# Two bf16 remainders of the weighed values moved from VectorE to GpSimd in layers 1 and 2

## The chip, the cores and the metric

The kernel runs on one core of a Trainium2 chip. The time is the device time of one execution in microseconds (us). The engines are named as in the profile: PE (TensorE, with PEld for its weight loads), DVE (VectorE), ACT (ScalarE), POOL (GpSimd) and SP (SyncE, whose queue issues the DMAs).

## What is computed

Eight graphs of 1024 nodes with 128 features pass through four layers, each behind a normalisation and with its input added at the end. Layers 1 and 2 are graph attention with additive scores, 4 and 8 heads:

```python
h = jnp.maximum(_layernorm(x, axis=-1), 0.0)
x = x + _L1_gnn_ref(h, adj, L1_gnn_W, L1_gnn_a)
h = jnp.maximum(_layernorm(x, axis=-1), 0.0)
x = x + _L2_gnn_ref(h, adj, adj[None], L2_gnn_W, L2_gnn_a_src, L2_gnn_a_dst, L2_gnn_beta_tilde, L2_gnn_W_out)
...
Wh = jnp.einsum('bnf,hfd->bhnd', x, W)
e = ei[:, :, :, None] + ej[:, :, None, :]
e = jnp.where(e > 0, e, ALPHA * e)
e = jnp.where(adj[None, None] > 0, e, MASK_VAL)
att = jax.nn.softmax(e, axis=-1)
h = jnp.einsum('bhij,bhjd->bhid', att, Wh)
```

Layer 0 is attention with dot products, layer 3 attention with a bilinear score. Neither is touched.

## The kernel before

**The idea of layers 1 and 2.** The exponential of a leaky relu of a sum of two terms is one of two products of a factor per row and a factor per column; which of the two holds depends on the sign of the sum. So no score matrix is exponentiated. Per head a matrix `g` of fp8 marks where the sum is positive and an edge exists; PE multiplies `g` with the node values weighed by the column factors (L1032, into `acc`), and the edge matrix alone with the other weighing (L1014, into `post`). The weighed values are float32, and PE reads them as three bf16 parts that sum to the float32 value: the upper half of the word, the upper half of what is left, and the upper half of what is left after that. They lie in `parts`, two buffers `parts0` and `parts1`, for graphs in turn.

**The steps that make the parts.** `dve_weigh` (L1143, L1145) writes part 0 and raises `vals_ready`. `dve_rest` (L1149) writes part 1, which is part 0 less its bf16 half, and raises `rest_ready`. `dve_last_rest` (L1153) writes part 2 in the same way from part 1 and raises `parts_ready`, on which PE waits ahead of the first head of the next graph. Each of the two is one subtraction over 128 x 2112 elements in layer 1 and 128 x 2176 in layer 2, float32 from one input, every second bf16 from the other, all in SBUF.

**The order of the work.** Each engine has its own order, written by hand in `additive_layers`: a loop over graphs, in it a loop over heads `h`, and between heads numbered slots, two per head. The tables `soon` and `later` say which step of the next graph and of the one after it is done in which slot. On DVE a graph of layer 1 is: for each head, the marks of the head after it (`dve_head`: L1171, which makes one tile in layer 1 and two in layer 2, and two L1181, which combine with the edges), the sums of the head before it from PSUM (`dve_sums`, L1188, which free the four banks of `acc`), and the slots. `dve_weigh` stands in slot 4 (slot 6 in layer 2), the end of the graph before (`dve_combine`, L1205 to L1219) behind head 1, and `dve_base` (L1196, reads `post`) behind heads 2 to 4. ACT makes the other tiles of `g` (L1097), from rows `s_all` that SP loads; SP sends the load of a head once DVE has done L1171 of the head two before. PE may run a head into a bank of `acc` only once DVE has read the head before out of it.

**POOL** does little: per graph `pool_rstd` (L116, L118: the scale and offset of the normalisation two graphs ahead, for ACT's L125) and `pool_top` (L967: a maximum over all partitions, from `top_part`, for DVE's L1131). Between L967 and another kind of instruction stands an instruction that the order calls ISA.

## Time and profile before

| | us |
|---|---|
| median of 3 runs (lowest, highest) | 2028.11 (2024.01, 2032.48) |
| the profiled execution | 2026.8 |
| its span | 2024.6 |
| DVE busy | 1603.9, 79% |
| PE busy | 1650.5, 82% |
| ACT busy | 1339.6, 66% |
| POOL busy | 126.2, 6% |

The span is what the trace covers; the execution is 2.2 us longer. Layers 1 and 2 run from about 700 to 1640 us in the span. A busy share is an average over stages with different limits, and PE's is over modelled ends of pipelined matmuls. In a row of the timeline, the first number is the start and the second the time from the start of the first to the end of the last instruction of the row, whose count stands at the end; in square brackets is how long the engine was idle before it and who ended that. Single DVE instructions of a row overlap their neighbours by some hundredths of a microsecond.

### The profile page before, as it was taken

To read this page: it belongs to the slowest core of one execution; us is meant where nothing else is said; L and a number is where in the kernel's file an instruction comes from. 1 tells how busy PE (TensorE), PEld (TensorE's weight loads), DVE (VectorE), ACT (ScalarE), POOL (GpSimd) and SP (SyncE) were. 2 spreads that over 40 slices of the span, in tenths; PEclk is the share of its full clock that TensorE was granted. 3 is DMA by queue.
4 is the path that set the end of the run, shared out by engine and by line. 5 is a ranking of instruction groups with operands and counts; after the bars stand their busy time and mean duration, and the time that the engine had idled before them with its cause. 6 is when DMAs were issued, how large, how long until landed. Compare 5 with 4: busy or idle time off the path is not lost. (4 is left out here: it accounts for less than half of the span.)

```text
span 2024.6 us, 36872 instructions
## 1 busy us (share of the span) xinstructions
PE 1650.5 (82%) x13620; PEld 1056.3 (52%) x13620; DVE 1603.9 (79%) x2710; ACT 1339.6 (66%) x1751; POOL 126.2 (6%) x130
## 2 busy tenths in 40 slices
PE   3998988988986577999999777977797748999997
PEld 1444443434433356777777556755675534555554
DVE  4888988988987557888888889898888747666764
ACT  2766666666663576777776989888888814554553
POOL 1000010010000100000000000000000000000000
PEclk7999999999998688999999878888888869999999
DMA  8634634635622311111111112111211120000000
GB/s 232 160 102 122 141 92 115 147 89 127 141 71 68 119 43 39 47 43 42 50 46 43 54 64 74 65 64 55 74 65 64 63 89 1 11 22 10 10 11 21
DMA packets 74922, 146.49 MB, mean 72 GB/s; under 512 B 11937, under 2 KB 34722, under 8 KB 74754
## 3 DMA queue, kind: packets, MB, share of 16 engines
q1 hardware_dynamic: 74754, 144.23, 25.4%
q8 instruction: 108, 1.77, 0.4%
q14 instruction: 60, 0.49, 0.1%
HBM read 101.85 MB, written 8.78 MB: 55 GB/s over the span
## 5 line engine op out<-in xcount | busy, mean ns | idle before, releaser
L1097 ACT ACTIVATE g<-s_all,steep_d 128x1024 fp8e4<-128x1024 f32 x608 | 642.3, 1135 | 40.6 <-DMA s_all<-s_rows 20.6
L1032 PE MATMUL acc<-parts,g 128*128 128x102 bf16 (+1 forms) x6144 | 417.2, 229 | 24.7 <-DVE sums L1188 24.5
L1032 PEld LDWEIGHTS acc<-parts,g 128*128 128x128 fp8e4 x6144 | 401.5, 100 | 57.4 <-issue 40.5
L1014 PE MATMUL post<-parts,edge 128*128 128x396 bf16 (+1 forms) x1024 | 233.7, 384 | 88.4 <-DVE base L1196 88.4
L583 ACT ACTIVATE e<-s_ps 128x1024 f32<-128x1024 f32 x256 | 248.1, 1022 | 24.5 <-PE s_ps L439 22.3
L1181 DVE TENSOR_TENSOR g<-g,edge 128x1024 int32<-128x1024 int32 x192 | 228.1, 1220 | 34.1 <-ACT g L1097 34.1
L732 DVE SCALAR_TENSOR_TENSOR e<-e,bound 128x1024 f32<-128x1024 f32 x160 | 191.0, 1228 | 43.4 <-ACT e L583 43.3
L1014 PEld LDWEIGHTS post<-parts,edge 128*128 128x128 fp8e4 x1024 | 102.5, 102 | 195.9 <-issue 111.5
L435 PE MATMUL s_ps<-qs,ks 128*128 128x512 f32 x512 | 193.5, 487 | 6.6 <-DMA ks<-split 4.9
L451 PE MATMUL sum_ps<-e,pick 128*32 128x256 f32 x2048 | 142.2, 396 | 67.6 <-DVE e L732 57.4
L1879 ACT ACTIVATE z<-z,shift 128x1024 f32<-128x1024 f32 x64 | 73.6, 1149 | 161.0 <-DVE shift L1955 161.0
L589 ACT ACTIVATE chunk<-ctx_ps 128x512 f32<-128x512 f32 x128 | 76.2, 595 | 136.0 <-PE ctx_ps L460 136.0
L435 PEld LDWEIGHTS s_ps<-qs,ks 128*128 128x128 f32 x512 | 94.4, 197 | 128.2 <-issue 70.1
L1188 DVE TENSOR_REDUCE sums<-acc 128x132 f32<-128x396 f32 (+1 forms) x256 | 133.9, 569 | 27.3 <-PE acc L1032 27.2
L460 PE MATMUL ctx_ps<-e,v 128*32 128x512 f32 x1024 | 140.1, 620 | 0.0
L451 PEld LDWEIGHTS sum_ps<-e,pick 128*32 128x32 f32 x2048 | 54.7, 111 | 137.7 <-DVE e L732 68.2
L1948 DVE CUSTOM_DVE_ANT_0 z<-s_ps,bias 128x1024 f32<-128x1024 f32 x64 | 78.4, 1225 | 60.7 <-PE s_ps L1786 60.4
L1786 PE MATMUL s_ps<-ht,q 128*128 128x512 f32 x256 | 121.8, 598 | 4.9 <-DVE top L1948 3.8
L1808 PE MATMUL o_ps<-zt,h 128*128 128x512 f32 x256 | 117.9, 604 | 6.0 <-ACT zt L1884 6.0
L125 ACT ACTIVATE h<-x,offset,rstd 128x128 f32<-128x128 f32 (+1 forms) x256 | 101.8, 482 | 30.7 <-POOL offset L118 30.7
L1171 DVE TENSOR_SCALAR g<-s_all,minus_d 128x1024 fp8e4<-128x1024 f32 x160 | 114.3, 748 | 8.4 <-issue 3.2
L133 PE MATMUL aux<-ident,h 128*128 128x128 f32 x256 | 42.6, 322 | 80.2 <-ACT h L125 80.2
(158 smaller groups left out, 2146.7 us busy)
## 6 DMA issues: line engine op xcount, KB each, us to landing
s_all<-s_rows SPq DMA_DIRECT2D x96, 512.0 KB, 3.7
inv_all<-inv_rows SPq DMA_DIRECT2D x256, 128.0 KB, 2.9
qs<-split SPq DMA_DIRECT2D x128, 128.0 KB, 3.2
ks<-split SPq DMA_DIRECT2D x128, 128.0 KB, 2.8
x<-in_x SPq DMA_DIRECT2D x8, 512.0 KB, 6.8
inv_rows<-inv SPq DMA_DIRECT2D x32, 128.0 KB, 1.8
adj_in<-in_adj SPq DMA_DIRECT2D x8, 512.0 KB, 4.1
out_x<-x SPq DMA_DIRECT2D x8, 512.0 KB, 3.2
```

The costliest lines, as they stand in the source:

```text
L435: ins = pe.matmul(s_ps[:, hp, j, :], ks[par][:, 2 * hp + j, jt * P:(jt + 1) * P], qs[par][:, 2 * hp + j, half * HALF:(half + 1) * HALF], s ...
L451: ins = pe.matmul(sum_ps[h * DH:(h + 1) * DH, :], pick[:, at:at + DH], e[:, 2 * (i % 2) + h // 2, h % 2, q * QUARTER:(q + 1) * QUARTER], s ...
L460: ins = pe.matmul(ctx_ps[h * DH:(h + 1) * DH, :], v[par][:, i % T, h * DH:(h + 1) * DH], e[:, 2 * (i % 2) + h // 2, h % 2, :], start=True, ...
L583: act.activation(e[:, 2 * (i % 2) + hp, :, :], s_ps[:, hp, :, :], ACT.Exp, scale=SCALE).then_inc(exp_done, 1)
L732: dve.scalar_tensor_tensor(out=tile, in0=tile, scalar=CLIP_LO, in1=lim, op0=ALU.max, op1=ALU.min).then_inc(p_ready, 1)
L1014: ins = pe.matmul(self.post[:, it % 2, 0:H * 3 * W1].rearrange("p (h k c) -> p h k c", h=H, k=3), self.c.edge[:, jt, it * P:(it + 1) * P], ...
L1032: ins = pe.matmul(self.acc[:, bank, o:o + self.NS], self.g[:, h % RING, jt, it * P:(it + 1) * P], self.upper[par][:, jt, h, :, :].rearrang ...
L1097: act.activation(self.g[:, h % RING, jt, :], self.s_all[:, h % 2, :], ACT.Relu, bias=self.steep_d[par][:, jt, h:h + 1], scale=STEEP, satur ...
L1181: dve.tensor_tensor(both, both, c.edge[:, some, :].rearrange("p t n -> p (t n)").bitcast(I32), ALU.bitwise_and).then_inc(self.g_ready, 1)
L1188: dve.tensor_reduce(self.sums[par][:, h, PER * k:PER * k + PER, :, :].rearrange("p i k c -> p i (k c)"), self.acc[:, (READS * h + k) % 4, ...
L1786: ins = pe.matmul(s_ps[:, j * HALF:(j + 1) * HALF], q[par][:, i * P:(i + 1) * P], ht[par][:, j * HALF:(j + 1) * HALF], start=True, stop=True)
L1808: ins = pe.matmul(o_ps[:, :], c.h[:, par, t, :], zt[:, quad, t, :], start=(t == 0), stop=(t == T - 1))
```

## The change

The two subtractions become `pool_rest` and `pool_last_rest`, with the same operands and the same semaphores, issued on GpSimd. Their slots on DVE go. On GpSimd they stand in the stage of graph b for graph b + 1, behind `pool_rstd` of graph b + 2 and ahead of `pool_top` of graph b + 2. `pool_rest` waits for `vals_ready` on its own, `pool_last_rest` for `rest_ready`.

```diff
-    def dve_rest(self, dve, n, par):
-        dve.wait_ge(self.vals_ready, n + 1)
-        dve.tensor_tensor(self.part(par, 1), self.part(par, 0), self.cut(par, 0), ALU.subtract).then_inc(self.rest_ready, 1)
-
-    def dve_last_rest(self, dve, n, par):
-        dve.wait_ge(self.rest_ready, n + 1)
-        dve.tensor_tensor(self.part(par, 2), self.part(par, 1), self.cut(par, 1), ALU.subtract).then_inc(self.parts_ready, 1)
+    def pool_rest(self, pool, n, par):
+        wait_apart(self.c, pool, self.vals_ready, n + 1)
+        pool.tensor_tensor(self.part(par, 1), self.part(par, 0), self.cut(par, 0), ALU.subtract).then_inc(self.rest_ready, 1)
+
+    def pool_last_rest(self, pool, n, par):
+        pool.wait_ge(self.rest_ready, n + 1)
+        pool.tensor_tensor(self.part(par, 2), self.part(par, 1), self.cut(par, 1), ALU.subtract).then_inc(self.parts_ready, 1)
...
                 one.pool_top(pool, 0)
+                one.pool_rest(pool, 0, 0)
+                one.pool_last_rest(pool, 0, 0)
                 one.pool_top(pool, 1)
 
             def stage(a, b, par):
-                at = ahead(a, b, par, 2)
+                at, soon = ahead(a, b, par, 2), ahead(a, b, par, 1)
                 if at:
                     at[0].pool_rstd(pool, at[1])
+                if soon:
+                    soon[0].pool_rest(pool, soon[1], soon[2])
+                    soon[0].pool_last_rest(pool, soon[1], soon[2])
+                if at:
                     at[0].pool_top(pool, at[1])
...
-                one.dve_rest(dve, 0, 0)
-                one.dve_last_rest(dve, 0, 0)
                 one.dve_sd(dve, 1, 1)
...
-            soon = {4: {2: [Additive.dve_zs], 4: [Additive.dve_weigh], 5: [Additive.dve_rest], 6: [Additive.dve_last_rest]},
-                    8: {2: [Additive.dve_zs], 6: [Additive.dve_weigh], 8: [Additive.dve_rest], 10: [Additive.dve_last_rest]}}
+            soon = {4: {2: [Additive.dve_zs], 4: [Additive.dve_weigh]},
+                    8: {2: [Additive.dve_zs], 6: [Additive.dve_weigh]}}
```

**GpSimd at the opening of layer 1, before.** These are its instructions from the first two graphs' scales to the third's; the names end in the layer.

```order
L967 ISA [waits top_partial1]
L967 ISA top1<-top_part1 128x4
L967 ISA top1<-top_part1 128x4 [waits top_partial1]
L116 ISA
L116 TENSOR_TENSOR rstd<-var_eps,mhalf 128x8 [waits var_done,h_ready]
L118 TENSOR_TENSOR offset<-minus_mean,rstd 128x8 [waits rstd_done]
```

The same place in the changed kernel, with the steady order of layer 1 from the second `L967 ISA` on:

```order
L967 ISA [waits top_partial1]
L967 ISA top1<-top_part1 128x4
L1149 ISA [waits vals_ready1]
L1149 TENSOR_TENSOR parts0_12<-parts0_12 128x32x66
L1153 TENSOR_TENSOR parts0_12<-parts0_12 128x32x66 [waits rest_ready1]
L967 ISA [waits top_partial1]
L967 ISA top1<-top_part1 128x4
L116 ISA
L116 TENSOR_TENSOR rstd<-var_eps,mhalf 128x8 [waits var_done,h_ready]
L118 TENSOR_TENSOR offset<-minus_mean,rstd 128x8 [waits rstd_done]
L1149 TENSOR_TENSOR parts1_12<-parts1_12 128x32x66 [waits vals_ready1]
L1153 TENSOR_TENSOR parts1_12<-parts1_12 128x32x66 [waits rest_ready1]
```

At the opening the two subtractions stand between two L967 that were neighbours, with two more ISA instructions; in every later stage they follow L118 with none.

**VectorE in a graph of layer 1**, from the weighing of the next graph's values to the reads of `post`, as one piece of the difference:

```order
 L1188 TENSOR_REDUCE sums1_12<-acc12 128x132 x4
-L1149 TENSOR_TENSOR parts0_12<-parts0_12 128x32x66
-L1196 TENSOR_REDUCE base12<-post12 128x132 x2
-L1153 TENSOR_TENSOR parts0_12<-parts0_12 128x32x66
-L1196 TENSOR_REDUCE base12<-post12 128x132 x2
+L1196 TENSOR_REDUCE base12<-post12 128x132 x4
```

What stood on both sides of the first reads of `post` is gone; everything ahead of it, the weighing (L1143, L1145), `dve_combine` (L1205 to L1219) and the next marks, is as it was.

## Rows read from the trace of the kernel before

**Rows 1.** Windows, one graph each: length; busy us (instructions) of PE, PEld, DVE, ACT, POOL; clock; DMA.

```profile
916.00:964.00 48.00, 43.47 (x363) 34.74 (x362) 42.60 (x76) 36.65 (x43) 2.96 (x3) 0.96 0.14 46
1446.00:1514.00 68.00, 53.87 (x684) 42.96 (x682) 60.13 (x95) 59.42 (x66) 2.93 (x3) 0.85 0.20 70
```

**Rows 2.** Waits of PE, 750 to 1640 us: total, times, longest.

```profile
PE post L1014 <- DVE base L1196: 88.4, 16, 11.8
```

**Rows 3.** Groups of DVE by shape, 700 to 1640 us: busy, mean ns, idle before.

```profile
L1149 DVE TENSOR_TENSOR parts<-parts 128x2176 f32<-128x2176 f32 x8 | 19.3, 2417 | 0.0
...
L1153 DVE TENSOR_TENSOR parts<-parts 128x2112 f32<-128x2112 f32 x8 | 18.8, 2350 | 0.0
```

**Rows 4.** Timeline of one graph of layer 1, 916 to 970 us.

```profile
930.32 0.22 DVE L1145 COPY parts<-keyf 128x64 f32<-128x64 f32 x1
930.42 1.25 DVE L1205 TENSOR_TENSOR sums<-base,sums 128x1056 f32<-128x1056 f32 x1
...
939.49 1.99 DVE L1188 TENSOR_REDUCE sums<-acc 128x132 f32<-128x396 f32 x4
...
943.36 3.02 PE L1032 MATMUL acc<-parts,g 128*128 128x198 bf16 x32
...
949.70 0.57 DVE L1196 TENSOR_REDUCE base<-post 128x132 f32<-128x396 f32 x1 [2.73 <-PE post L1014]
```

**Rows 5.** Timeline of one graph of layer 2, 1375 to 1455 us.

```profile
1402.08 0.29 DVE L1145 COPY parts<-keyf 128x128 f32<-128x128 f32 x1
...
1405.38 1.41 DVE L1171 TENSOR_SCALAR g<-s_all,minus_d 128x1024 fp8e4<-128x1024 f32 x2
...
1411.40 0.58 DVE L1188 TENSOR_REDUCE sums<-acc 128x136 f32<-128x408 f32 x1 [1.85 <-PE acc L1032]
...
1412.62 3.60 PE L1014 MATMUL post<-parts,edge 128*128 128x408 bf16 x16 [0.37 <-DVE base L1196]
```

**Rows 6.** Timeline of DVE in layer 0, around a copy on POOL.

```profile
177.34 1.22 DVE L732 SCALAR_TENSOR_TENSOR e<-e,bound 128x1024 f32<-128x1024 f32 x1
...
178.48 1.63 DVE L732 SCALAR_TENSOR_TENSOR e<-e,bound 128x1024 f32<-128x1024 f32 x1
```

**Rows 7.** Timeline of POOL in layer 0: a rstd, and that copy.

```profile
143.20 2.48 POOL L116 TENSOR_TENSOR rstd<-var_eps,mhalf 128x8 f32<-128x8 f32 x1 [27.34 <-DVE var_eps L111]
...
177.42 1.60 POOL L385 COPY late<-h 128x512 f32<-128x512 f32 x1
```

**Rows 8.** Timeline of DVE beside that rstd.

```profile
144.22 1.23 DVE L755 TENSOR_TENSOR ctx_sb<-ctx_sb,weighed 128x1024 f32<-128x1024 f32 x1
```

**Rows 9.** Timeline, 916 to 970 us: POOL's maximum, and what it waits for.

```profile
916.40 0.39 POOL L967 PARTITION_ALL_REDUCE top<-top_part  x1 [38.41 <-issue]
...
923.63 2.20 POOL L116 TENSOR_TENSOR rstd<-var_eps,mhalf 128x8 f32<-128x8 f32 x1 [6.85 <-issue]
...
957.99 0.21 DVE L1121 TENSOR_REDUCE top_part<-sd 128x4 f32<-128x32 f32 x1
...
964.41 0.39 POOL L967 PARTITION_ALL_REDUCE top<-top_part  x1 [38.12 <-issue]
```

**Rows 10.** Timeline of the opening of layer 1, 686 to 730 us.

```profile
696.05 0.22 DVE L1145 COPY parts<-keyf 128x64 f32<-128x64 f32 x1
...
704.87 5.86 PE L1032 MATMUL acc<-parts,g 128*128 128x198 bf16 x64
...
713.85 1.70 POOL L116 TENSOR_TENSOR rstd<-var_eps,mhalf 128x8 f32<-128x8 f32 x1 [11.35 <-DVE var_eps L111]
...
718.15 3.17 ACT L125 ACTIVATE h<-x,offset,rstd 128x128 f32<-128x128 f32 x8
...
719.89 8.18 PE L1032 MATMUL acc<-parts,g 128*128 128x198 bf16 x64 [9.16 <-DVE sums L1188]
```

**Rows 11.** Timeline, 916 to 970 us: PE behind a wait for ACT.

```profile
929.66 1.93 PE L133 MATMUL aux<-ident,h 128*128 128x128 f32 x8 [4.27 <-ACT h L125]
...
931.38 6.70 PE L1032 MATMUL acc<-parts,g 128*128 128x198 bf16 x64
```

## The prediction

> **What bounds the kernel now.** I read first one graph of each of the two layers by windows [rows 1]. In layer 1 a graph takes 48 us, PE is busy 43.5 of them and VectorE 42.6; in layer 2 it takes 68 us, VectorE is busy 60.1 and ScalarE 59.4. So VectorE is nearly full in both, and work taken from it looks welcome. A share does not say where the work is late, so the waits of PE come next: it waits 88.4 us for VectorE's reads of `post` [rows 2]. Those reads stand ahead of the place from which the two subtractions are taken. The timeline decides. In layer 1 the four reads of `acc` start at 939.49, the first ends 0.5 us later, about 940.0, and frees the bank that PE enters at 943.36: 3.4 us to spare. The subtractions follow these reads, and soon after VectorE waits 2.73 us for PE [rows 4]. In layer 2, PE waits for VectorE's read at 1412.62 [rows 5]; the first subtraction of the graph follows that read, too. So what is removed, two times 2.35 us in layer 1 and two times 2.42 in layer 2 [rows 3], stands where PE has already got what it needs. I cost its removal at nothing in layer 1, and at a gain of nothing to 2.4 us a graph in layer 2, of which I take nothing, since VectorE's next waits there are for PE.
>
> **What is added: two long reads by GpSimd beside a full VectorE.** The trace has no GpSimd subtraction of this size. It has a copy of 128x512, issued at 177.42, while VectorE is in an instruction with two inputs from SBUF that ends at 178.56. The copy ends at 179.02, 0.46 us later. The VectorE instruction that starts at 178.48 takes 1.63 us, its twin ahead of it 1.22 [rows 6, 7]. So GpSimd waited for VectorE's instruction, then VectorE for GpSimd, by 0.41 us. A `rstd` of 8 elements takes 2.48 us, and the VectorE instruction beside it an undisturbed 1.23 [rows 7, 8]: what holds VectorE up is GpSimd's reading, not its computing.
>
> How long does one of the new instructions hold it, call it D? The copy gives 0.41/512 = 0.80 ns for an element of one input; two inputs of 2112 elements give 3.4 us, the lower bound. The whole 1.60 us of the copy, waiting included, scaled to 2112 elements is 6.6 us, the upper bound. I take 4.0 us: near the lower end, because 1.14 of the copy's 1.60 us lie ahead of 178.56 and are mostly its wait; somewhat above it, because a subtraction has to bring two inputs together, one of them read at every second element, where the copy had one dense one.
>
> The Trainium skill (SBUF — State Buffer, Who interferes with whom) says that a GpSimd instruction that reads SBUF and a VectorE instruction with two SBUF inputs, or in a two-port mode, exclude each other, and that whichever starts first holds the port for its whole instruction. The copy's rows agree; the `rstd` does not bear out the whole instruction. The skill's GPSIMD Engine Reference, Elementwise side by side, has 4497 ns for an add of 2048 float32 elements; by it D would be an estimated 4.6 us and the sum below 94 us in place of 77.
>
> **Layer 1, graphs with a `dve_combine` ahead of them: 7.** `vals_ready` comes at 930.54, when L1205 has begun, which has two SBUF inputs, as have the L1208 and L1211 behind it [rows 4]. GpSimd's first subtraction gets in at the end of L1205, holds VectorE for D, the second waits for one VectorE instruction and holds it for D again. Everything behind it, the next marks and the reads of `acc` among them, comes 2D = 8.0 us later. 3.4 of that is PE's spare time [rows 4], so PE stalls 4.6 us. Nothing on PE's side takes that back: the rest of its graph shifts, and ScalarE, which has time to spare in this layer [rows 1], shifts with it. VectorE's removed 4.7 us come after the harm and only fill VectorE's waits. A PE that has waited is slower behind it: 64 equal matmuls take 5.86 us, behind a wait of 4.27 us 6.70, and behind one of 9.16 us 8.18 [rows 10, 11]. The granted clock is 0.96 in this graph and 0.85 in layer 2, where PE waits more [rows 1]. I add 1.5 us, between 0.8 and 2.3. Sum: 7 x (4.6 + 1.5) = 43 us. The first stage of layer 1 has no `dve_combine`; it goes with the opening.
>
> **Layer 2: 7 graphs.** `vals_ready` comes at 1402.37, while VectorE only reads PSUM and waits for PE, up to 1405.38. The first D lies from 1402.6 to 1406.6 and costs 1.2 us. The first L1171 runs to 1407.3, the second D to 1411.3, and the pair of L1171 ends at 1412.0 in place of 1406.8, 5.2 us later. VectorE's wait of 1.85 us for PE ahead of the read at 1411.40 takes up its part, and the read for which PE waits at 1412.62 comes 3.4 us late [rows 5]; in D it is 2D - 4.6. ScalarE has little room in this layer and gets the delay from PE through the ring of `g`, so I let it stand: 7 x 3.4 = 24 us. The last of these has an ISA ahead of its subtraction and comes later; the same price is taken.
>
> **The opening: 10 us.** In the steady stages the subtractions follow L118 with no ISA. At the opening one stands ahead of L1149, one ahead of the second L967, and one is there as before ahead of L116. What it costs: from the end of L967 at 916.79 to L116 it is 6.8 us, with `var_eps` long there, and from `top_part` at 958.20 to L967 it is 6.2 us [rows 9]. So GpSimd starts L1149 at 696.27 + 6.8 = 703.1, is done with both at 712.3 (8.0 and a VectorE instruction of 1.2 between them), runs L967 at 718.5 to 718.9 and L116 at 725.7 in place of 713.85; with its 1.70 and L118's 0.6 us, ScalarE's L125 starts at 728.2 in place of 718.15 [rows 10]. PE's first head moves from 704.87 to 712.4, which its wait of 9.16 us behind it covers. ScalarE's 10 us are not covered: its next tiles are what VectorE and PE wait for there.
>
> **Queues.** On GpSimd the subtractions stand behind `rstd` two graphs ahead, so ScalarE's L125 is not held up, and ahead of the next L967, whose `top_part` comes 27 us after `vals_ready` (958.20 against 930.54). `parts_ready` comes by about 942 in layer 1, and PE asks for it only at the next graph's first head, behind all of this graph's; no wait there. SP's queue loads `s_all` once L1171 is done, which comes later with the rest of VectorE.
>
> **The sum.** 10 + 43 + 24 = 77 us on the profiled execution's 2026.8 (2024.6 of span and 2.2 around it) is 2104; the median of the runs is 1.3 us above that execution, so I forecast 2105 us. With D = 3.4 it is 9 + 7 x (3.4 + 0.8) + 7 x 2.2 = 54 us, 2082. With D = 6.6 it is 15 + 7 x (9.8 + 2.3) + 7 x 8.6 = 160 us, 2188.
>
> **Rivals.** (a) GpSimd's reads slip in between VectorE's and hold nothing up. For it speaks that the only disturbance seen is one of 0.41 us behind a short copy, and the undisturbed 1.23 beside the `rstd`; against it, that 0.41 is just what a held port would cost for 512 elements. It decides at D below 1.7 us in layer 1 (3.4/2) and 2.3 in layer 2. Then only the opening's 10 us stay, less a few from layer 2: 2033 us, no change that can be told. (b) They hold VectorE, but give way after each of its instructions, so that a D of 4.0 costs some 2.4: 7 x (1.4 + 0.8) + 7 x 0.2 + 8 = 25 us, 2053. (c) The subtraction is slow on GpSimd (two inputs, one of them every second bf16), D from 5 up: 2140 to 2190. (d) The other side: nothing is held up, and VectorE's freed 4.8 us shorten each graph of layer 2, since its busy share is the highest there: 7 x 4.8 = 34 us less the opening's 10, 2004. Against it speak rows 5: the read for which PE waits comes before the freed time. It would need PE's later waits to go to VectorE.
>
> **How the numbers follow.** Forecast 0.60 (2080 to 2125), (a) 0.14, (b) 0.10, (c) 0.12, (d) 0.04. A measurement of this kernel can tell about 0.5%, 10 us, from no change. Faster 0.04, within 0.14, slower 0.82. The range of 2032 to 2150 leaves out (d), half of (a) and the upper half of (c), some 0.17.
>
> **What would show it.** In the changed kernel: GpSimd's L1149 and L1153 last 4 to 6 us each. In layer 1 the L1208 and L1211, of L1205's kind and size (1.25 us), take 4 to 6, PE has a new wait for VectorE's L1188 of 4 to 5 us a graph, and a graph takes 54 us in place of 48. In layer 2 an L1171 is stretched to 4 to 5 us and PE's waits for L1196 grow. At the opening, rstd starts at about 725. I am wrong if L1208 takes about 1.25 us, if the new instructions last under 2 us, or if they start only after VectorE has gone through L1215, as they would if VectorE always went first.

## The result, and the profile after

| | before | changed |
|---|---|---|
| median of the runs | 2027.53 us (4 runs, 2024.01 to 2032.48) | 2081.52 us (4 runs, 2078.56 to 2084.17) |
| ratio, 95% interval | | 1.0264, 1.0237 to 1.0291 |
| profiled execution, span | 2026.8, 2024.6 | 2082.91, 2081.1 |
| POOL busy | 126.2 us | 260.8 us |
| DVE busy | 1603.9 us | 1616.5 us |

The change makes the kernel 54 us slower. The forecast was 2105 us, the range 2032 to 2150, so the measured time lies 23 us below the forecast, inside the range. The first thing to see in the page of the changed kernel is VectorE: two times sixteen subtractions have been taken from it, some 76 us, and it is busy longer than before.

```profile
PE 1677.8 (81%) x13620; PEld 1070.2 (51%) x13620; DVE 1616.5 (78%) x2678; ACT 1340.9 (64%) x1751; POOL 260.8 (13%) x162
```

The instructions themselves, by source line (minimum, median and maximum in ns). A subtraction takes 3.71 us in layer 1 and 3.81 in layer 2 where nothing disturbs it:

```profile
L1149 POOL TENSOR_TENSOR parts<-parts x16: 3703/3816/4597, 705.4 to 1597.9; 128x2112 f32<-128x2112 f32 x8, 128x2176 f32<-128x2176 f32 x8
L1153 POOL TENSOR_TENSOR parts<-parts x16: 3706/4142/4707, 709.4 to 1601.8; 128x2112 f32<-128x2112 f32 x8, 128x2176 f32<-128x2176 f32 x8
```

And the groups of VectorE by shape, 700 to 1700 us. The work of L1208 and L1211 is the same in both layers, up to 3% in size. In layer 2 it stands where GpSimd does no subtraction:

```profile
L1171 DVE TENSOR_SCALAR g<-s_all,minus_d 128x1024 fp8e4<-128x1024 f32 x160 | 148.3, 960 | 10.1 <-issue 3.9 <-DVE x L1228 2.7 <-PE acc L1032 2.5
...
L1208 DVE TENSOR_TENSOR sums<-sums,ratio 128x1056 f32<-128x1056 f32 x8 | 34.1, 4256 | 0.3
L1211 DVE TENSOR_TENSOR sums<-sums 128x1056 f32<-128x1056 f32 x8 | 33.9, 4236 | 0.3
...
L1208 DVE TENSOR_TENSOR sums<-sums,ratio 128x1088 f32<-128x1088 f32 x8 | 10.3, 1291 | 0.3
```

**Where the time went.** GpSimd's instructions cut the layers into the same stretches in every kernel: from the first L116 to the third L967 (opening), from there to the tenth (stages 1 to 7 of layer 1), on to the sixteenth (stages 0 to 5 of layer 2), and on to the first L116 after it (the rest of layer 2). Worked out from the starts in the two timelines, in us:

| | opening | layer 1 | layer 2 | its end | sum |
|---|---|---|---|---|---|
| before | 101.6 | 339.0 | 404.2 | 136.6 | 981.4 |
| changed | 112.3 | 371.8 | 413.6 | 137.2 | 1034.9 |
| difference | +10.7 | +32.8 | +9.4 | +0.6 | +53.5 |

**Layer 1.** The timeline of one graph, the counterpart of [rows 4]:

```profile
954.75 1.25 DVE L1205 TENSOR_TENSOR sums<-base,sums 128x1056 f32<-128x1056 f32 x1
955.05 4.52 POOL L1149 TENSOR_TENSOR parts<-parts 128x2112 f32<-128x2112 f32 x1 [4.43 <-DVE parts L1145]
...
955.75 7.25 PE L1032 MATMUL acc<-parts,g 128*128 128x198 bf16 x64
956.03 4.64 DVE L1208 TENSOR_TENSOR sums<-sums,ratio 128x1056 f32<-128x1056 f32 x1
959.65 4.60 POOL L1153 TENSOR_TENSOR parts<-parts 128x2112 f32<-128x2112 f32 x1
960.71 0.23 ACT L1085 ACTIVATE ratio<-z_ratio 128x32 f32<-128x32 f32 x1 [3.66 <-DVE sums L1208]
960.71 4.64 DVE L1211 TENSOR_TENSOR sums<-sums 128x1056 f32<-128x1056 f32 x1
...
966.06 3.42 PE L165 MATMUL aux<-wv,h_t 128*128 128x128 f32 x16 [3.07 <-ACT h_t L138]
...
972.45 3.02 PE L1032 MATMUL acc<-parts,g 128*128 128x198 bf16 x32
...
978.79 0.57 DVE L1196 TENSOR_REDUCE base<-post 128x132 f32<-128x396 f32 x1 [5.26 <-PE post L1014]
```

GpSimd's subtraction starts at 955.05, loses 0.81 us to L1205 (4.52 against 3.71), and then holds L1208: 4.64 us against L1205's 1.25 for the same shape and layer 2's 1.29. With the undisturbed 1.26 of an L1208 of this shape, D, the time for which one GpSimd subtraction holds VectorE up, is 3.38 us. The next pair repeats it. So far it is the predicted picture. But in this graph the delay does not reach PE at L1032: when PE comes to the bank (972.45, no wait in brackets), it has already been delayed elsewhere. The delay comes by ScalarE. Its L1085 overwrites `ratio`, which L1208 reads, so it waits 3.66 us for L1208, and L138 stands behind it in ScalarE's order; L138 makes the transposed input for PE's L165. The same two steps in the kernel before:

```profile
933.00 0.23 ACT L1085 ACTIVATE ratio<-z_ratio 128x32 f32<-128x32 f32 x1 [0.27 <-DVE sums L1208]
...
938.35 2.05 PE L165 MATMUL aux<-wv,h_t 128*128 128x128 f32 x16 [0.27 <-ACT h_t L138]
```

PE waits 3.07 us at L165 where it waited 0.27, and its work on both sides is slower (the granted clock of the graph is 0.90 for 0.96): 7.25 us for 64 matmuls that took 6.70 [rows 11], 3.42 for the sixteen of L165 that took 2.05. 2.80 + 0.55 + 1.37 = 4.7 us, most of the 5.0 us by which the graph is longer (53.0 us in place of 48.0), as the windows show (length; PE, PEld, DVE, ACT, POOL busy; clock). The first is the counterpart of the layer 1 window in [rows 1]; the second is the graph of layer 2 that comes ahead of the one in [rows 1], and took 69.3 us before:

```profile
940.80:993.80 53.00, 45.67 (x366) 36.80 (x364) 45.07 (x74) 36.76 (x43) 11.91 (x6) 0.90 0.13 41
1428.30:1499.90 71.60, 54.92 (x648) 43.30 (x645) 60.86 (x93) 57.76 (x65) 11.60 (x5) 0.83 0.18 61
```

Of the seven stages with a `dve_combine`, six take 4.8 to 6.4 us longer, 33.2 us in sum. In five of them PE waits for L138, 3.07 to 3.92 us. In the last of the six it waits 3.57 us for L1188, at 1131.82, the way that the prediction named. The first of the seven is not longer (from L967 to L967 48.5 us, 48.9 before): there PE stands 9.60 us behind ScalarE's late L125, as it did before (11.2 us), and the stretched L1208 lies under that.

```profile
793.60 3.70 POOL L1149 TENSOR_TENSOR parts<-parts 128x2112 f32<-128x2112 f32 x1
793.60 4.81 DVE L1208 TENSOR_TENSOR sums<-sums,ratio 128x1056 f32<-128x1056 f32 x1
...
797.00 1.94 PE L133 MATMUL aux<-ident,h 128*128 128x128 f32 x8 [9.60 <-ACT h L125]
```

PE's waits, 700 to 1700 us (total, times, longest). Of those in [rows 2], 88.4 has become 103.2. The third line is the way just described; it was 1.7 us before. The wait for L1188 (second line) was 24.5 us before, over the whole stretch:

```profile
PE post L1014 <- DVE base L1196: 103.2, 16, 11.6
...
PE acc L1032 <- DVE sums L1188: 25.9, 7, 8.9
...
PE aux L165 <- ACT h_t L138: 17.6, 5, 3.9
```

**Layer 2.** The counterpart of [rows 5]:

```profile
1383.85 3.81 POOL L1149 TENSOR_TENSOR parts<-parts 128x2176 f32<-128x2176 f32 x1 [12.64 <-DVE parts L1145]
...
1386.64 5.79 DVE L1171 TENSOR_SCALAR g<-s_all,minus_d 128x1024 fp8e4<-128x1024 f32 x2
...
1387.74 4.14 POOL L1153 TENSOR_TENSOR parts<-parts 128x2176 f32<-128x2176 f32 x1
...
1396.31 4.58 PE L1014 MATMUL post<-parts,edge 128*128 128x408 bf16 x16 [2.80 <-DVE base L1196]
```

The first subtraction ends at 1387.66, beside VectorE's PSUM reads and the start of the L1171 pair. The second gets in ahead of the pair's second instruction, and the pair takes 5.79 us in place of 1.41: 4.4 us. PE's wait for the read of `post` is 2.80 us where it was 0.37 [rows 5]; [rows 5] are of the next graph, but this wait was 0.36 to 0.37 in each of the first six graphs of layer 2, and is 2.5 to 3.5 in each of them now. In the seventh, the loop's end, it is 1.26 both times.

**The opening.** The counterpart of [rows 10]:

```profile
689.51 0.39 POOL L967 PARTITION_ALL_REDUCE top<-top_part  x1 [11.44 <-issue]
...
705.37 3.90 POOL L1149 TENSOR_TENSOR parts<-parts 128x2112 f32<-128x2112 f32 x1 [15.47 <-issue]
...
709.35 4.03 POOL L1153 TENSOR_TENSOR parts<-parts 128x2112 f32<-128x2112 f32 x1
...
713.79 8.61 PE L1032 MATMUL acc<-parts,g 128*128 128x198 bf16 x64 [8.06 <-issue]
...
719.26 0.39 POOL L967 PARTITION_ALL_REDUCE top<-top_part  x1 [5.87 <-issue]
...
726.70 2.10 POOL L116 TENSOR_TENSOR rstd<-var_eps,mhalf 128x8 f32<-128x8 f32 x1 [7.06 <-issue]
...
729.12 3.19 ACT L125 ACTIVATE h<-x,offset,rstd 128x128 f32<-128x128 f32 x8 [8.66 <-POOL offset L118]
```

Each of the three switches between L967 and another kind of instruction costs the path some 6 to 7 us, in a row: ahead of L1149 (a fill at the same place, e5 below, starts at 698.4), from the end of L1153 at 713.38 to 719.26, and on to L116 at 726.70. ScalarE's L125 waits for all of them. It starts 11.0 us later than before; 1.7 us of that is there already when the layer begins (670.94 for 669.24), 9.3 us is the opening's.

### The profile page after: what moved, and what is told of

Its sections match the earlier page's. It is cut to its first block and busy times, and to the rows that moved or that the text cites. A ratio compares the mean times of both kernels' runs of the same rounds, so it can differ in the third digit from the quotient of the medians.

```text
span 2081.1 us, 36896 instructions
## 1 busy us (share of the span) xinstructions
PE 1677.8 (81%) x13620; PEld 1070.2 (51%) x13620; DVE 1616.5 (78%) x2678; ACT 1340.9 (64%) x1751; POOL 260.8 (13%) x162
## 5 line engine op out<-in xcount | busy, mean ns | idle before, releaser
L1032 PE MATMUL acc<-parts,g 128*128 128x102 bf16 (+1 forms) x6144 | 423.3, 230 | 37.8 <-DVE sums L1188 25.9
L1032 PEld LDWEIGHTS acc<-parts,g 128*128 128x128 fp8e4 x6144 | 406.1, 100 | 72.7 <-issue 54.8
L1014 PE MATMUL post<-parts,edge 128*128 128x396 bf16 (+1 forms) x1024 | 244.8, 398 | 103.2 <-DVE base L1196 103.2
L583 ACT ACTIVATE e<-s_ps 128x1024 f32<-128x1024 f32 x256 | 248.2, 1022 | 24.5 <-PE s_ps L439 21.6
L1181 DVE TENSOR_TENSOR g<-g,edge 128x1024 int32<-128x1024 int32 x192 | 231.2, 1237 | 36.8 <-ACT g L1097 36.8
L1014 PEld LDWEIGHTS post<-parts,edge 128*128 128x128 fp8e4 x1024 | 106.2, 106 | 218.1 <-issue 142.5
L1188 DVE TENSOR_REDUCE sums<-acc 128x132 f32<-128x396 f32 (+1 forms) x256 | 133.8, 568 | 33.0 <-PE acc L1032 32.9
L1171 DVE TENSOR_SCALAR g<-s_all,minus_d 128x1024 fp8e4<-128x1024 f32 x160 | 148.3, 960 | 10.1 <-issue 3.9
L116 POOL TENSOR_TENSOR rstd<-var_eps,mhalf 128x8 f32<-128x8 f32 x32 | 64.4, 2011 | 648.9 <-DVE var_eps L111 547.5
L1196 DVE TENSOR_REDUCE base<-post 128x132 f32<-128x396 f32 (+1 forms) x128 | 69.7, 569 | 73.1 <-PE post L1014 71.8
L125 ACT ACTIVATE h<-x,offset,rstd 128x128 f32<-128x128 f32 (+1 forms) x256 | 101.8, 482 | 38.1 <-POOL offset L118 38.1
```

What stands on the lines that cost most here:

```text
L583: act.activation(e[:, 2 * (i % 2) + hp, :, :], s_ps[:, hp, :, :], ACT.Exp, scale=SCALE).then_inc(exp_done, 1)
L1014: ins = pe.matmul(self.post[:, it % 2, 0:H * 3 * W1].rearrange("p (h k c) -> p h k c", h=H, k=3), self.c.edge[:, jt, it * P:(it + 1) * P], ...
L1032: ins = pe.matmul(self.acc[:, bank, o:o + self.NS], self.g[:, h % RING, jt, it * P:(it + 1) * P], self.upper[par][:, jt, h, :, :].rearrang ...
L1171: dve.tensor_scalar(self.g[:, h % RING, jt, :], self.s_all[:, h % 2, :], self.minus_d[par][:, jt, h:h + 1], EDGE, ALU.is_gt, ALU.mult, sat ...
L1181: dve.tensor_tensor(both, both, c.edge[:, some, :].rearrange("p t n -> p (t n)").bitcast(I32), ALU.bitwise_and).then_inc(self.g_ready, 1)
L1188: dve.tensor_reduce(self.sums[par][:, h, PER * k:PER * k + PER, :, :].rearrange("p i k c -> p i (k c)"), self.acc[:, (READS * h + k) % 4, ...
```

## The experiments

The theory was that GpSimd's reading of two inputs holds VectorE for D, at the place where the subtraction falls, and that this place decides what it costs. The rivals were that the time goes elsewhere: into the removal, into GpSimd's slowness for PE, into writes, or into the opening alone. The table gives for each kernel the stretches defined above, from its profiled execution. What the texts on record call the theory and the rival is said in each.

| | median, us | ratio to before (95%) | opening | layer 1 | layer 2 | its end |
|---|---|---|---|---|---|---|
| before | 2023 to 2028 | | 101.6 | 339.0 | 404.2 | 136.6 |
| changed | 2081.52 | 1.0264 (1.0237, 1.0291) | 112.3 | 371.8 | 413.6 | 137.2 |
| e1 removed only | 2017.64 | 0.9955 (0.9932, 0.9977) | 101.9 | 339.0 | 385.0 | 132.4 |
| e2 added only | 2098.71 | 1.0368 (1.0340, 1.0396) | 112.7 | 371.8 | 429.1 | 139.8 |
| e3 first graph back | 2071.42 | 1.0230 (1.0206, 1.0255) | 105.7 | 371.6 | 412.4 | 136.3 |
| e4 layer 2 only | 2037.37 | 1.0059 (1.0037, 1.0082) | 101.8 | 339.1 | 411.5 | 137.6 |
| e5 writes only | 2005.35 | 0.9901 (0.9874, 0.9928) | 101.7 | 339.0 | 385.0 | 133.1 |
| e6 one input | 2017.23 | 0.9967 (0.9950, 0.9984) | 102.4 | 353.3 | 383.9 | 133.2 |
| e7 ratio behind h_t | 2077.65 | 1.0260 (1.0231, 1.0288) | 113.2 | 368.3 | 413.2 | 135.4 |
| e8 placed | 2015.04 | 0.9961 (0.9947, 0.9974) | 101.6 | 339.0 | 396.5 | 131.2 |
| e9 placed, base moved | 2012.50 | 0.9941 (0.9927, 0.9955) | 101.7 | 339.5 | 401.0 | 124.2 |
| e10 before, base moved | 1997.34 | 0.9862 (0.9847, 0.9877) | 101.3 | 341.0 | 382.1 | 127.3 |
| e11 last one placed | 1992.27 | 0.9833 (0.9811, 0.9856) | 101.4 | 339.5 | 378.1 | 125.8 |
| e12 last graph back | 1991.52 | 0.9833 (0.9809, 0.9857) | 101.8 | 339.0 | 378.8 | 125.4 |

### The two halves of the change: e1 and e2

e1 is the kernel before, its two subtractions cut to one row, except for the first two graphs of each layer.

```diff
     def dve_rest(self, dve, n, par):
         dve.wait_ge(self.vals_ready, n + 1)
-        dve.tensor_tensor(self.part(par, 1), self.part(par, 0), self.cut(par, 0), ALU.subtract).then_inc(self.rest_ready, 1)
+        few = slice(0, None) if isinstance(n, int) and n < 2 else slice(0, 1)
+        dve.tensor_tensor(self.part(par, 1)[:, few, :], self.part(par, 0)[:, few, :], self.cut(par, 0)[:, few, :],
+                          ALU.subtract).then_inc(self.rest_ready, 1)
```

> The kernel before with VectorE's two subtractions cut to one row of 66 or 34 elements in every graph but the first two of each layer (parts 1 and 2 of those graphs are left out of the computation), nothing on GpSimd. Theory (what is removed stands in VectorE's slack): the time of before within 5 us, 2022 to 2030, although VectorE is freed of 12 x 4.75 = 57 us. Rival (VectorE's load is the bound, and the changed kernel is slower only because GpSimd's share costs more than the removal brings): 30 to 57 us faster, 1970 to 1998.

Measured: 2017.64 us in the median of nine executions, 4 us below the theory's range and 20 above the rival's; they lie between 2004.31 and 2020.07, and the profiled one is the fastest of them. Layer 1 is the same to 0.1 us. There VectorE's removed time is worth nothing, as costed. In layer 2 the profiled execution gains 19 us, and 4 more in its end; by the median it is 6 us in all. How much of it stays in an ordinary execution, this run does not settle. e5 below, which frees VectorE of all sixteen pairs, has the same 385.0 us in layer 2, and all four of its executions are 16 us or more below before.

e2 is the kernel before, with both subtractions on VectorE, and two more on GpSimd at the places of the change, with the same inputs, into a tile that nobody reads.

```diff
+    def pool_spare(self, pool, n, par):
+        wait_apart(self.c, pool, self.vals_ready, n + 1)
+        to = self.spare[:, 0:T * self.H * 2 * self.W1].rearrange("p (a b) -> p a b", a=T * self.H)
+        for k in range(2):
+            pool.tensor_tensor(to, self.part(par, 0), self.cut(par, 0), ALU.subtract).then_inc(self.spared, 1)
+            pool.wait_ge(self.spared, 2 * n + k + 1)
```

> The kernel before, unchanged on VectorE, with two subtractions of the same size and inputs on GpSimd at the places of the change, written to a spare tile. Theory (the cost is all in the adding, VectorE held 3.4 us each time): about the changed kernel's time, 2075 to 2090, L1208 and L1211 in layer 1 at 4.6 us. Rival (the removal gave something back in the changed kernel): clearly above it, 2095 to 2130.

Measured: 2098.71 us, 9 to 24 above the 2075 to 2090 of the theory. Opening and layer 1 are those of the changed kernel to 0.4 us: there the harm is all in what is added, and nobody waits for its result. Layer 2 and its end are 18 us above the changed kernel (15.5 and 2.6), so inside the change, the removal does give something back there, some 2.6 us for each of 7 graphs. (The time itself, 2098.71, lies in the rival's range.) VectorE's own two subtractions read two inputs as well, but they are hardly held in e2, 0.7 us in sum over layer 2, so that is not where the 18 us come from. For layer 1 the theory held, for layer 2 the rival.

### What holds VectorE: e5 and e6

e5 lets GpSimd fill the two parts with zeros at the same places: it writes as much and reads nothing. e6 lets it copy: one float32 input in place of two inputs.

```diff
     def pool_rest(self, pool, n, par):
         wait_apart(self.c, pool, self.vals_ready, n + 1)
-        pool.tensor_tensor(self.part(par, 1), self.part(par, 0), self.cut(par, 0), ALU.subtract).then_inc(self.rest_ready, 1)
+        pool.memset(self.part(par, 1), 0.0).then_inc(self.rest_ready, 1)
```

```diff
-        pool.tensor_tensor(self.part(par, 1), self.part(par, 0), self.cut(par, 0), ALU.subtract).then_inc(self.rest_ready, 1)
+        pool.tensor_copy(self.part(par, 1), self.part(par, 0)).then_inc(self.rest_ready, 1)
```

> The changed kernel with both GpSimd subtractions replaced by a fill with zero of the same elements (parts 1 and 2 are left out of the computation): no reading, as much writing. Theory (it is GpSimd's reading that holds up VectorE's second input): L1208 and L1211 at their 1.26 us, the one-input L1171 in layer 2 perhaps held by the writing, and of the loss only the opening stays, 2030 to 2042. Rival (any GpSimd instruction of this size holds VectorE for its whole length): L1208 stretched by the fill's length, 2050 or more.

> The changed kernel with both GpSimd subtractions replaced by a copy of the float32 input (parts 1 and 2 are not the remainders): half of the reading. Theory (0.80 ns for an element read, so VectorE is held 1.7 us in place of 3.4): L1208 and L1211 at about 2.95 us in layer 1; 2 x 1.7 is just PE's 3.4 us to spare, so the graphs cost nothing and the opening stays, 2033 to 2045. Rival (held for the whole instruction with its computing, the same for one input as for two): L1208 at about 4.6 us and 2070 to 2085.

VectorE's L1208 by source line (minimum, median, maximum in ns), of the changed kernel, of e5 and of e6, one fence for each:

```profile
L1208 DVE TENSOR_TENSOR sums<-sums,ratio x16: 1258/1292/4814, 793.6 to 1686.2; 128x1056 f32<-128x1056 f32 x8, 128x1088 f32<-128x1088 f32 x8
```

```profile
L1208 DVE TENSOR_TENSOR sums<-sums,ratio x16: 1257/1276/1293, 783.1 to 1609.2; 128x1056 f32<-128x1056 f32 x8, 128x1088 f32<-128x1088 f32 x8
```

```profile
L1208 DVE TENSOR_TENSOR sums<-sums,ratio x16: 1257/1292/2965, 780.9 to 1621.3; 128x1056 f32<-128x1056 f32 x8, 128x1088 f32<-128x1088 f32 x8
```

Writing holds it not at all, one input by 1.64 us in most graphs (1.70 at most), two by 3.38, which is twice that. 2112 times the 0.80 ns that one element of one input cost in the kernel before [rows 6, 7] is 1.69. So D goes by the elements read, and that the bf16 operand lies at every second place adds nothing that can be seen. These two runs alone would also fit a hold for the length of any instruction that reads, less some 0.3 us, since the copy is about half as long as the subtraction (1.95 us and 3.71). Against that stands the `rstd` of 8 elements, 2.48 us long, beside which VectorE ran undisturbed [rows 7, 8].

The Trainium skill (SBUF — State Buffer, Who interferes with whom) has the first of the two hold the port for its whole instruction, and has a GpSimd instruction that only writes not disturb a VectorE instruction with two SBUF inputs. This case's traces agree for these instructions: of the changed kernel's 3.71 us VectorE is held for 3.38, and beside the fill of e5, 1.86 us, an L1208 takes its 1.26.

In time, e5 took 2005.35 us, 18 less than before and 25 less than the 2030 that its expectation had at the least. e6 took 2017.23, 16 below its own. Both expectations had left two things out. The opening did not stay as in the changed kernel, it went back to 101.7 and 102.4: a fill or a copy needs no switch behind L967, and e5's L1149 starts at 698.4, in place of 705.4. And in layer 2 VectorE's freed time is worth 19 and 20 us when nothing holds VectorE for long (385.0 and 383.9 us in place of 404.2). e6 shows one more thing. Nothing was expected in layer 1, since 2D = 3.4 just fits into the 3.4 us of spare time at the bank [rows 4]. It cost 14 us there:

```profile
938.82 2.90 DVE L1208 TENSOR_TENSOR sums<-sums,ratio 128x1056 f32<-128x1056 f32 x1
...
941.75 0.23 ACT L1085 ACTIVATE ratio<-z_ratio 128x32 f32<-128x32 f32 x1 [1.91 <-DVE sums L1208]
...
947.10 2.05 PE L165 MATMUL aux<-wv,h_t 128*128 128x128 f32 x16 [2.03 <-ACT h_t L138]
```

The way by ScalarE has nearly no spare time: L1208's 1.64 us of delay is there again as PE's 2.03. It is the way that e7 tests.

### The way to PE in layer 1: e7

The changed kernel, but in the stages with a `dve_combine` of layer 1 ScalarE does L138 a slot earlier, and L1085, which waits for L1208, a slot later, behind it.

```diff
+            soon_7 = {4: {1: [Additive.act_wh], 5: [Additive.act_row], 6: [Additive.act_exps], 8: [Additive.act_ratios]},
+                      8: soon[8]}
+            later_7 = {4: {6: [Additive.act_h], 7: [Additive.act_h_t]}, 8: later[8]}
```

> The changed kernel, but in layer 1 ScalarE's step L1085, which waits for VectorE's L1208, stands half a head later and the copy L138, for which PE waits 3.1 us a graph in the changed kernel, half a head earlier. Theory (two waits of the same size lie side by side: when PE no longer waits for L138, it waits for VectorE's L1188 to free the bank of acc, as the prediction had it): the time within 5 us of the changed kernel, 2076 to 2086, with the wait moved to L1188. Rival (ScalarE's wait for L1208 is the only way by which the delay reaches PE): 15 to 25 us below the changed kernel.

Measured: 2077.65 us, 4 below the changed kernel, with layer 1 3.5 us shorter. PE's waits, 700 to 1700 us, of this kernel; that for L138 has gone from the list:

```profile
PE post L1014 <- DVE base L1196: 105.3, 16, 12.2
...
PE acc L1032 <- DVE sums L1188: 46.0, 13, 8.9
```

The wait for L1188 has grown from 25.9 us and 7 times to 46.0 and 13 times. All six of the longer stages of layer 1 now have one, of 2.92 to 5.40 us, 4.0 in the mean, where the changed kernel had it in one of them (3.57 us). The prediction's 2D - 3.4 gives 3.4 with the measured D. So the two ways stand side by side: one D less some 0.3 us by ScalarE, two D less 3.4 by the bank. With D = 3.38 they are about equal, PE comes first to the one by ScalarE, and taking that away uncovers the other.

### It goes by place: e3, e4 and e8

e3 is the changed kernel with the first graph's two subtractions back on VectorE; e4 has them on GpSimd in layer 2's stages alone.

```diff
                 one.pool_top(pool, 0)
-                one.pool_rest(pool, 0, 0)
-                one.pool_last_rest(pool, 0, 0)
                 one.pool_top(pool, 1)
...
                 one.dve_weigh(dve, 0, 0)
+                one.dve_rest(dve, 0, 0)
+                one.dve_last_rest(dve, 0, 0)
                 one.dve_sd(dve, 1, 1)
```

> The changed kernel, but the first graph of layer 1, ahead of the loops, has its subtractions on VectorE. Theory (the opening costs about 10 us through the two ISA instructions, which put rstd at 727): 10 us below the changed kernel, 2069 to 2074, rstd at about 714. Rival (the opening's delay is lost in waits further on): within 3 us of the changed kernel, 2078 to 2084.

> Subtractions on GpSimd in the stages of layer 2 alone (7 graphs), the 9 of layer 1's stages on VectorE. Theory (the cost goes by place, about 1.6 us a graph there as the changed kernel's trace has it): 9 to 13 us above before, 2037 to 2041. Rival (every pair of subtractions costs alike, 54/16 = 3.4 us): 24 us above, 2051.

e3: 2071.42 us, 10 less than changed, in the 2069 to 2074 expected, with the `rstd` at 713.32. The opening is 6.6 us shorter, the other stretches 0.2 to 1.2. 4.1 us of the opening's 10.7 stay. Since e4, with none on GpSimd in layer 1, is at 101.8, they come from the second graph's subtractions in stage 0. e3's timeline shows the way:

```profile
725.09 7.87 DVE L1189 TENSOR_TENSOR g<-g,edge 128x1024 int32<-128x1024 int32 x2 [1.43 <-ACT g L1097]
...
733.58 4.44 PE L1032 MATMUL acc<-parts,g 128*128 128x198 bf16 x32 [2.87 <-DVE sums L1196]
```

(L1189 and L1196 are L1181 and L1188 there.) The two L1181 lie beside the subtractions, the reads of `acc` behind them come late, and PE has a wait of 2.87 us for them that the kernel before does not have. It is the way by the bank that the prediction named for the later graphs.

e4: 2037.37 us, in the 2037 to 2041 expected; opening and layer 1 are those of before. Of its price (14 us by the medians), the stretches of the profiled execution show 8.6: 7.3 in layer 2, 1.0 in its end, 0.3 elsewhere.

e8 moves GpSimd's instructions away from VectorE's two-input instructions. The first graph's two are back on VectorE, as in e3. In layer 1 GpSimd's two wait until the marks of the last head are made, behind which VectorE reads PSUM and waits for PE; in layer 2 the second one waits until the marks of the next graph's first head are made.

```diff
                 if soon:
+                    if a.H == 4:
+                        pool.wait_ge(a.g_ready, 2 * a.H * b + 8)
                     soon[0].pool_rest(pool, soon[1], soon[2])
+                    if a.H == 8:
+                        wait_apart(c, pool, soon[0].g_ready, 2 * soon[0].H * soon[1] + 2)
                     soon[0].pool_last_rest(pool, soon[1], soon[2])
```

> The changed kernel with the first graph on VectorE and GpSimd made to wait: in layer 1 with both subtractions until VectorE has done the marks of the graph's last head, in layer 2 with the second until the marks of the next graph's first head are done, so that GpSimd reads while VectorE mostly reads PSUM or waits. Theory (only the place costs): within 8 us of before, 2020 to 2036, L1208 at 1.26 us. Rival (GpSimd's reading costs wherever it stands): 2060 to 2075.

Measured: 2015.04 us, 0.4% faster than before, and 5 us below the theory's range. GpSimd's instructions by source line are undisturbed, and in layer 1 so is VectorE; in layer 2 some of its L1171 still take up to 2.26 us for 0.75:

```profile
L1149 POOL TENSOR_TENSOR parts<-parts x15: 3709/3805/3817, 729.1 to 1533.1; 128x2176 f32<-128x2176 f32 x8, 128x2112 f32<-128x2112 f32 x7
```

Layer 1's stretch costs what it did before (339.0): same instructions, same count, same engine, and the 32.8 us are gone. It settles for layer 1 that neither GpSimd's slowness nor the number of its instructions is the cause, but what VectorE does at the time. In layer 2 it gains 7.7 us and 5.4 at the end, though PE there waits once, 4.8 us in the last graph, for GpSimd's L1153.

### A faster kernel: e9 to e12

In layer 2 PE's largest wait is for VectorE's reads of `post` [rows 2], which stood behind heads 2 to 4. e10 is the kernel before with the first two of them moved up, behind `dve_combine`, and the next two a slot earlier, ahead of the weighing, and nothing on GpSimd; e9 is e8 with the same move.

```diff
                     if h == 2:
-                        a.dve_base(dve, b, (0, 1))
+                        a.dve_base(dve, b, (0, 1) if a.H == 4 else (2, 3))
...
-                    if h == 2:
+                    if h == 2 and a.H == 4:
                         a.dve_base(dve, b, (2, 3))
...
                         before[0].dve_combine(dve, before[1], before[2])
+                        if a.H == 8:
+                            a.dve_base(dve, b, (0, 1))
```

> The kernel of e8, and in layer 2 VectorE reads the first two tiles of post (L1196) right behind dve_combine, two steps earlier, and the next two ahead of the weighing. PE waited 8 to 11 us a graph for the first of these reads, before and after the change. Theory (layer 2 is bound by the chain of VectorE steps up to these reads, so its time comes back only when they come earlier): 10 to 25 us below e8 and below both kernels, 1990 to 2005, PE's waits for L1196 down from 88 us in total to below 50. Rival (ScalarE, busy 87% in layer 2, binds as soon as PE does not wait): within 5 us of e8, 2010 to 2020.

> The kernel before with the same move of the reads of post in layer 2, and nothing on GpSimd. Theory: 10 to 20 us below before, 2003 to 2013; what e9 has on top of it, 5 to 12 us, is what the placed subtractions on GpSimd are worth. Rival (the subtractions on VectorE fill room that ScalarE's bound leaves anyway): within 3 us of e9.

Measured: e10 1997.34 us, better than the 2003 to 2013 expected; e9 2012.50, above the 1990 to 2005 of its theory and inside its rival's 2010 to 2020. PE's waits for these reads are 57 us in sum in e10 and 76 in e9, for 88 before; below 50 was expected. So with the reads moved, the kernel without GpSimd is 15 us the faster of the two, and the sign of e8 has turned. The timeline of e9, in layer 2:

```profile
1402.52 4.97 DVE L1179 TENSOR_SCALAR g<-s_all,minus_d 128x1024 fp8e4<-128x1024 f32 x2
1402.85 4.09 POOL L1149 TENSOR_TENSOR parts<-parts 128x2176 f32<-128x2176 f32 x1 [15.80 <-DVE parts L1145]
...
1411.38 4.58 PE L1014 MATMUL post<-parts,edge 128*128 128x408 bf16 x16 [5.08 <-DVE base L1204]
1411.51 6.36 ACT L1097 ACTIVATE g<-s_all,steep_d 128x1024 fp8e4<-128x1024 f32 x6 [4.16 <-DMA s_all<-s_rows]
```

(L1179 and L1204 are L1171 and L1196 there.) The move shifted `vals_ready`, and with it GpSimd's first subtraction, straight onto the pair of marks, which takes 4.97 us for 1.41. What waits is PE, and ScalarE too: SP's load of a head stands behind those marks, and ScalarE waits 4.16 us for it.

e11 tests that reading: e10, with the last subtraction of layer 2 alone on GpSimd, in e8's place, and the first on VectorE.

```diff
-                    8: {2: [Additive.dve_zs], 6: [Additive.dve_weigh], 8: [Additive.dve_rest], 10: [Additive.dve_last_rest]}}
+                    8: {2: [Additive.dve_zs], 6: [Additive.dve_weigh], 8: [Additive.dve_rest]}}
...
+                if soon and a.H == 8:
+                    wait_apart(c, pool, soon[0].g_ready, 2 * soon[0].H * soon[1] + 2)
+                    soon[0].pool_last_rest(pool, soon[1], soon[2])
```

> The kernel before, with layer 2's reads of post moved as in the run that beat both kernels (1997 us), and of all the subtractions one kind alone on GpSimd: the last one (L1153) of layer 2's graphs 1 to 7, which waits until the marks of the next graph's first head are made. The first subtraction and all of layer 1 stay on VectorE. Theory: where both were on GpSimd with the moved reads (2012 us), the loss against 1997 came from the first subtraction, which fell on VectorE's L1171, and the last one, in its place, is free, since VectorE has the PSUM reads there. Then this gives 1997 us or up to 10 less (seven times 0 to 1.4 us of the 2.42 us taken from VectorE), 1987 to 1999, and no L1171 over 2 us. Rival: the placed subtraction itself costs what its removal brings, since it holds VectorE for about 3.4 us against the 2.42 us removed wherever it falls on an instruction with two SBUF inputs: 2000 to 2010.

Measured: 1992.27 us, 20 below e9 and 5 below e10, in the theory's range and out of the rival's. Layer 2 is 4.0 us shorter than in e10, its end 1.5. One part of the expectation failed, that no L1171 would be over 2 us: in the last graph, where no graph follows, the order of the loop's end lets GpSimd fall on one, and PE waits for it, by the timeline of e11 (L1175 and GpSimd's L1149 are L1171 and L1153 there):

```profile
1545.89 3.80 POOL L1149 TENSOR_TENSOR parts<-parts 128x2176 f32<-128x2176 f32 x1 [54.87 <-DVE g L1185]
1545.89 5.02 DVE L1175 TENSOR_SCALAR g<-s_all,minus_d 128x1024 fp8e4<-128x1024 f32 x2
...
1550.14 6.14 PE L1032 MATMUL acc<-parts,g 128*128 128x102 bf16 x96 [11.72 <-POOL parts L1149]
```

e12 takes it away: the last graph's subtraction is on VectorE again.

```diff
+def is_last(n):
+    return isinstance(n, int) and n == B - 1
...
-                if soon and a.H == 8:
+                if soon and a.H == 8 and not is_last(soon[1]):
```

> The run before this one (1992 us), with the last graph's subtraction back on VectorE, in slot 10, so that GpSimd makes the last parts of layer 2's graphs 1 to 6 alone. In that run PE waited once for GpSimd, 11.72 us, in the last graph, where the loop goes straight from the marks of the last graph's first head to that head, and the subtraction held one L1171 (a pair of 1.41 us took 5.02). Theory: that wait was on the path, and all of it beyond what PE waits there anyway goes, with the stretched L1171: 5 to 9 us less, 1983 to 1987. Rival: PE waits at that place for something else just as long (the loop's last stage has VectorE late in any case): 1990 to 1994, no change.

Measured: 1991.52 us (1988.31 to 1995.66), the same. The rival was right: a wait of 11.72 us was worth nothing that can be told, and the end of layer 2, in which it lies, is 0.4 us shorter. The timeline of e12 shows what PE waits for instead (L1196 and L1204 are L1188 and L1196 there):

```profile
1529.15 31.30 ACT L1097 ACTIVATE g<-s_all,steep_d 128x1024 fp8e4<-128x1024 f32 x30 [0.70 <-issue]
...
1543.64 2.88 PE L1032 MATMUL acc<-parts,g 128*128 128x102 bf16 x32 [3.14 <-DVE sums L1196]
...
1556.56 3.90 PE L1014 MATMUL post<-parts,edge 128*128 128x408 bf16 x11 [4.94 <-DVE base L1204]
```

At the end of layer 2 ScalarE makes thirty tiles of `g` without a pause. PE's wait for GpSimd is gone, and it waits in several pieces for VectorE instead (3.14 and 4.94 us are two of them). The likeliest reading is that ScalarE's tiles set the end in both; that was not tested by itself. e11 and e12 beat both kernels of this case by 1.7% and 4.3%; e10, with those reads moved and nothing else, has most of that.

## Why the prediction was right, and where it was off

**What is added holds VectorE: right.** L1208 and L1211 are stretched to 4.64 us; the only rows of before that spoke of it were those of a copy and its neighbour [rows 6, 7]. With that (a) and (d) fall as wholes (of (d), the worth of the freed time in layer 2 is taken up below), and (b) too, since each pair is held for its whole D and GpSimd does not give way in between. (c) falls with D = 3.38.

**D: mis-sized, 4.0 for 3.38.** The lower bound, 0.80 ns for an element of one input, was the value (e5, e6). The addition for bringing two inputs together, one of them strided, had no row, and there is no such cost in the holding; it is in the instruction, 3.71 us for 3.38, where it harms nobody. With D = 3.4 the prediction's own sum is 54 us and 2082, what was measured. The estimate of 4.6 from the Trainium skill (GPSIMD Engine Reference, Elementwise side by side, 4497 ns for an add of 2048 elements) is too long for this instruction: 3.71 us for 2112.

**Layer 1: size right for D = 3.4, the way wrong.** 7 x (3.4 + 0.8) = 29 was given, 32.8 measured. The named wait, PE for L1188, hardly grew in sum (24.5 to 25.9), and of the six longer stages only the last has it (3.57 us). The step that failed is "3.4 of that is PE's spare time ... PE stalls": it looked at one reader of VectorE's work, the bank, and took it that ScalarE "shifts with it". ScalarE's L1085 waits for L1208 itself, and has nearly no spare time before PE's L165. e7 shows the bank behind it, with 4.0 us a wait, so the sum came out near by a coincidence of two prices: at D = 1.7 (e6) the prediction's formula gives 0 and the runs 14 us. A stretch was also counted in the first of the seven stages, which cost nothing, since PE waits there for L125 in any case (9.60 us, and 11.2 before); the six others cost 5.5 each in place of the 4.2 of the D = 3.4 sum, most of the difference being PE's slower work on both sides of its wait (0.55 and 1.37 us in the graph shown, taken at 0.8 together).

**Layer 1, removal at nothing: right.** e1 and e2 both show it, to 0.1 us.

**Layer 2: 24 for 9.4 and 0.6 at the end.** The mechanism was right: an L1171 pair at 5.79 us (predicted 1.41 + 5.2), PE later at L1014. Two terms were off. D = 3.38 brings the 24 down to 15. And the removal, "a gain of nothing to 2.4 us a graph, of which I take nothing", gives some 2.6 within the change (e2 against changed), so the added part alone is 24.9 + 3.2 = 28 us, 4.0 a graph, and more than the 2.2 of the formula; the two errors offset each other in part. Where little or nothing holds VectorE (e6, e5), layer 2 is 20 and 19 us shorter than before, 2.9 and 2.7 a graph, above the "nothing to 2.4". The reason given for nothing, that VectorE's next waits are for PE, did not exclude a gain: by the order of the instructions a later read, for which PE waits, stands behind them. That this read is the way was not tried by itself.

**The opening: 10 for 10.7, right in GpSimd's steps.** The predicted steps were L1149 at 703.1, L967 at 718.5, L116 at 725.7 and L125 at 728.2, on a kernel whose layer began at 669.24; this one's began at 670.94, 1.7 later. Measured 705.37, 719.26, 726.70 and 729.12, that is 703.7, 717.6, 725.0 and 727.4 on the scale of before. e3 shows the share of the first graph's subtractions, 6.6 us, where the prediction had all ten on GpSimd's order; the other 4.1 belong to the second graph's, in stage 0, for which the prediction had no price. The total came out near with one step too large and one left out.

**Queues: right.** L125 was not delayed past the opening, PE waited for `parts_ready` only at the opening (713.79, behind L1153's end at 713.38), as predicted, and L967 came in time.

**The signs.** L1149 and L1153 were said to last 4 to 6 us; 3.71 undisturbed, 4.5 to 4.6 beside VectorE, so the lower end was missed. A graph of layer 1 took 53 to 55 us (54 said). PE's new wait for L1188 came in one of the graphs of layer 1 only, as above.

## What to carry to other kernels

Moving work from a full engine to an idle one is not free where the two exclude each other at the memory: count what the new instruction reads, look up which instruction of the other engine stands at that moment, and follow everyone who waits for that one (not only the reader that you know). Then place it: the same pairs of subtractions cost 33 us in layer 1 behind `vals_ready`, and nothing beside reads of PSUM (e8). Before giving work away at all, see whether one read stands later in its engine's order than it needs to: a move of four short reads a graph (e10, 28 us) was worth more than all placing of GpSimd's work (e8, 9 us).

## What the runs showed of the hardware

- GpSimd holds VectorE's instructions with two inputs from SBUF for 0.80 ns for each element that it reads (128 partitions): 3.38 us for two inputs of 2112, up to 1.70 for one. An L1171, which has one large SBUF input, was held as well: the one that starts at 1388.13 in the changed kernel took 4.30 us for 0.75. Beside VectorE, GpSimd loses time as well, 4.52 and 4.60 us for 3.71.
- A fill by GpSimd, which reads nothing, does not hold such instructions (1.26 us), but does stretch some of L1171 (TENSOR_SCALAR, one SBUF input, fp8 output): by the source line of e5, up to 2.32 us against 0.75. Why the two kinds of VectorE instruction differ in this was not tried.

```profile
L1171 DVE TENSOR_SCALAR g<-s_all,minus_d x160: 733/746/2320, 702.9 to 1599.4; 128x1024 fp8e4<-128x1024 f32 x160
```

- The switch on GpSimd between L967's kind and a subtraction or the `rstd` costs 6 to 7 us each way, and a fill or a copy needs none: the openings of e5 and e6 are at 101.7 and 102.4 us, where the subtraction has 112.3.
- Left open: e1's nine executions spread from 2004 to 2020 us, with a granted clock of 0.921 and 0.923 in the two fastest and 0.910 to 0.914 in the five slowest, where the four of e5, whose VectorE is freed of all sixteen pairs (e1: of twelve), lie between 1999 and 2007. What the trace of one execution shows in layer 2 is no proof for the median there.
